# One hybrid layer on one core: the feed-forward variances on GpSimd, the channel mixes and three feed-forwards summed by VectorE, and new orders

## The reference, cut to what matters

```python
x = hidden                                     # (8, 512, 128): 8 batches, 512 tokens, 128 channels
n = layernorm(x);  q = n @ W_q.T               # attention without softmax
x = x + (q @ n.T) @ n
x = x + ffn(layernorm(x))
x = x + rwkv_block(layernorm(x))               # token mix (a scan over tokens), then channel mix
x = x + ffn(layernorm(x))                      # the same weights as the first feed-forward
def ffn(y):                                    # only expert 0 has weight
    z = y + relu(y @ w1 + b1) @ w2 + b2
    return (z - mean(z)) * rsqrt(var(z) + 1e-5) * gamma + beta
def channel_mix(x, xc):                        # second half of the rwkv block
    k = square(relu(mix(xc) @ Wk.T))
    return x + sigmoid(mix(xc) @ Wr.T) * (k @ Wv.T)
```

## Time and profile before

| what | value |
|---|---|
| median of 3 runs | 259.32 us |
| the profiled execution's own time | 259.21 us |
| its span | 257.4 us |
| TensorE busy | 249.5 us, 97% |
| VectorE busy | 231.2 us, 90% |
| ScalarE busy | 231.9 us, 90% |
| GpSimd busy | 133.2 us, 52% |
| granted TensorE clock | 0.997 of full |

### The profile page before, as it was taken

The page is one execution under the profiler, slowest core; times in us unless marked ns, Lnnn a source line. Parts: engine busy times, 40 slices in busy tenths (PEclk is TensorE's granted clock), DMA queues, the critical chain, the costliest instruction groups (busy, mean ns, idle before and its releaser), DMA issues.

```text
span 257.4 us, 5284 instructions
## 1 busy us (share of the span) xinstructions
PE 249.5 (97%) x1504; PEld 187.8 (73%) x1504; DVE 231.2 (90%) x757; ACT 231.9 (90%) x477; POOL 133.2 (52%) x258
## 2 busy tenths in 40 slices
PE   7899999999999999999999999999999999999991
PEld 7687778768767777668759767757848849778771
DVE  5897999999999999999999999999999995955454
ACT  3789789999999999999999999999999999895741
POOL 1656585944961974044596646636604525340640
PEclk9999999999999999999999999999999999999998
DMA  7932224013022240020763422205204424374297
GB/s 196 308 99 45 42 42 84 0 28 56 3 40 43 41 84 1 0 45 0 134 105 52 74 48 45 42 0 98 67 0 85 81 56 70 55 144 87 45 187 179
DMA packets 17772, 18.10 MB, mean 70 GB/s; under 512 B 1488, under 2 KB 11600, under 8 KB 17744
## 3 DMA queue, kind: packets, MB, share of 16 engines
q0 software_dynamic: 6480, 11.80, 27.0%
q1 hardware_dynamic: 10848, 5.84, 8.1%
q10 hardware_dynamic: 416, 0.14, 0.2%
HBM read 3.87 MB, written 2.10 MB: 23 GB/s over the span
## 4 chain that ended last, share of the span: by engine, by line
PE 94%; DVE 2%; DMA 1%; ACT 1%; POOL 1%; issue 0%; DVEq 0%; POOLq 0%; ACTq 0%
PE bank L1155 21%; PE bank L1164 21%; PE bank L1232 11%; PE bank L1226 11%; PE bank L1114 7%; PE bank L1213 3%; PE bank L1243 3%; PE bank L1197 3%; PE bank L1207 3%; PE bank L1202 3%; PE bank L1142 3%; PE bank L1127 2%; PE bank L1275 1%; DMA R<-in_hidden 1%; PE bank L1175 1%; PE bank L1135 1%
## 5 line engine op out<-in xcount | busy, mean ns | idle before, releaser
L1164 PEld LDWEIGHTS bank<-W,f_h 128*128 128x128 f32 x480 | 58.2, 192 | 8.7 <-issue 8.6
L1155 PE MATMUL bank<-f_yT,W 128*128 128x512 f32 x128 | 61.2, 593 | 0.0
L1164 PE MATMUL bank<-W,f_h 128*128 128x128 f32 x480 | 60.2, 275 | 0.0
L1155 PEld LDWEIGHTS bank<-f_yT,W 128*128 128x128 f32 x128 | 21.9, 190 | 16.3 <-issue 11.3
L1232 PEld LDWEIGHTS bank<-FWv,KK 128*128 128x128 f32 x256 | 30.6, 192 | 3.4 <-issue 2.3
L1226 PE MATMUL bank<-XK,FWk 128*128 128x512 f32 x64 | 32.0, 597 | 0.0
L1232 PE MATMUL bank<-FWv,KK 128*128 128x128 f32 x256 | 31.8, 275 | 0.0
L828 ACT ACTIVATE f_y<-R,f_yn_nb,f_yn_rs 128x128 f32<-128x128 f32 x64 | 26.3, 490 | 0.9 <-POOL f_yn_nb L350 0.9
L895 ACT ACTIVATE f_h<-bank,B 128x512 f32<-128x512 f32 x32 | 21.2, 681 | 5.5 <-PE bank L1155 4.2
L390 POOL DMA_DIRECT2D R<-G x7 | 6.3, 897 | 36.4 <-DVE G L686 36.4
L895 ACT ACTIVATE f_h<-bank,B1C 128x512 f32<-128x512 f32 x32 | 21.4, 682 | 0.1
(11 more groups left out here) (159 smaller groups left out, 620.3 us busy)
## 6 DMA issues: line engine op xcount, KB each, us to landing
R<-BETA POOLq DMA_DIRECT2D x16, 256.0 KB, 3.6
R<-f_zg POOLq DMA_DIRECT2D x14, 256.0 KB, 4.0
R<-N POOLq DMA_DIRECT2D x8, 256.0 KB, 3.4
R<-in_hidden SPq DMA_DIRECT2D x7, 256.0 KB, 5.0
R<-G POOLq DMA_DIRECT2D x7, 256.0 KB, 3.4
out_x<-R SPq DMA_DIRECT2D x7, 256.0 KB, 2.3
W<-in_w SPq DMA_DIRECT2D x2, 256.0 KB, 4.5
BETA<-in_beta SPq DMA_DIRECT2D x1, 256.0 KB, 4.6
```

Source lines behind the costliest of these rows:

```text
L1155: t_.matmul(banks[bank][:], W1[:, n * P:(n + 1) * P], at(f.yT, b)[:], start=True, stop=True).then_inc(f.h_psum[n], 1)
L1164: last = t_.matmul(banks[bank][:, j * C:(j + 1) * C], at(f.h, b)[:, n, j * P:(j + 1) * P], W2[:, n, :], start=False, stop=(n == H - 1), sk ...
```

## The change

It does four things.

1. `mean_var` of the 15 unsplit z goes from VectorE. In its place GpSimd runs `z_spread`: four small instructions that join the two halves of `bn_stats` to C times the variance. The logarithm reads that with `scale=1/C`. The wait of `z_stats` for its buffer is now on that step.
2. The seven accumulating DMAs of the channel mix and three of the feed-forwards (batch 4 of f1, batches 5 and 6 of f2) go from GpSimd's queue. VectorE adds instead: `cmix_out` for all batches, and a new `ffn_add`.
3. All four lists (GpSimd, VectorE, ScalarE, TensorE) have a new order and new banks. No matmul is added or removed.
4. One constant tile more is set at the start, so that the count waited for goes from 8 to 9.

```diff
-ADDED = {"f1": (0,), "f2": (7,), "x3": (7,)}
+ADDED = {"f1": (0, 4), "f2": (5, 6, 7), "x3": tuple(range(BATCHES))}
...
+            def z_spread(b, n):
+
+                pool.wait_ge(n.stats_done, b + 1)
+                if b >= 2:
+                    pool.wait_ge(*n.scale.done(b - 2, "ve"))
+                st = n.stats[b % 2]
+                pool.tensor_tensor(n.pair[b % 2][:], st[:, :, 1], st[:, :, 4], ALU.mult).then_inc(n.scale.sem(b), 1)
+                pool.tensor_tensor(n.sum[b % 2][:], st[:, :, 2], st[:, :, 5], ALU.add)
+                pool.wait_ge(*n.scale.done(b, "pair"))
+                pool.tensor_tensor(n.pair[b % 2][:], n.pair[b % 2][:], K_C[:], ALU.mult).then_inc(n.scale.sem(b), 1)
+                pool.wait_ge(*n.scale.done(b, "scaled"))
+                pool.tensor_tensor(n.spread[b % 2][:], n.sum[b % 2][:], n.pair[b % 2][:], ALU.subtract).then_inc(n.scale.sem(b), 1)
...
-            def cmix_sum(b):
-
-                pool.wait_ge(*cgate.done(b, "kvs"))
-                pool.wait_ge(*x2u.ready(b))
-                for earlier in x3.before(b):
-                    pool.wait_ge(*earlier)
-                pool.dma_start(R[b][:], at(G2, b)[:].rearrange("p (j c) -> p j c", j=J), accum_op=ALU.add).then_inc(*x3.step(b))
...
+            def ffn_add(b, f, tile):
+
+                dve.wait_ge(f.zg_ready, b + 1)
+                dve.wait_ge(*f.xb.ready(b))
+                v.tensor_tensor(R[b][:], at(tile, b)[:], R[b][:], ALU.add).then_inc(*f.out.step(b))
...
-                act.wait_ge(n.mv_ready, b + 1)
+                act.wait_ge(*n.scale.done(b, "spread"))
...
-                a.activation(n.ve[b % 2][:], n.mv[b % 2][:, :, 1], ACT.Ln, bias=K_EPS[:, 0:1]).then_inc(n.scale.sem(b), 1)
+                a.activation(n.ve[b % 2][:], n.spread[b % 2][:], ACT.Ln, bias=K_EPS[:, 0:1], scale=1.0 / C).then_inc(n.scale.sem(b), 1)
```

The beginning and the end of TensorE's list, the beginning of GpSimd's and the end of ScalarE's and VectorE's, which the prediction follows:

```diff
-            attn_transpose(0, 0); attn_gram(0, 1); attn_proj(0, 1); attn_apply(0, 1); attn_transpose(1, 0)
-            attn_gram(1, 2); attn_transpose(2, 1, x1.ready(0)); attn_proj(1, 2); attn_gram(2, 3); bias_rows()
-            attn_apply(1, 2); attn_transpose(3, 1); attn_proj(2, 3); attn_gram(3, 4)
-            ffn_transpose(0, f1, 2, x1.ready(1)); attn_apply(2, 3); hidden_up(0, f1, 0, 2)
+            attn_gram(0, 0); attn_transpose(0, 1); attn_proj(0, 0); attn_apply(0, 0); attn_transpose(1, 1)
+            attn_gram(1, 2); attn_transpose(2, 0, x1.ready(0)); attn_proj(1, 2); attn_gram(2, 3); attn_apply(1, 2)
+            attn_proj(2, 3); bias_rows(); ffn_transpose(0, f1, 0); attn_apply(2, 3); hidden_up(0, f1, 1, 0)
...
-            power(3, na); shift(0, f1.norm); bias(3, na); power(0, f1.norm); bias(0, f1.norm); shift(1, f1.norm)
+            power(3, na); shift(0, f1.norm); power(0, f1.norm); bias(0, f1.norm); shift(1, f1.norm); power(1, f1.norm)
...
-            proj_evacuate(0, 1); attn_normed(1); attn_normed(2); gram_evacuate(1, 2); attn_evacuate(1, 0)
-            attn_evacuate(2, 1); proj_evacuate(1, 2); attn_normed(3); gram_evacuate(2, 3); ffn_normed(0, f1)
+            proj_evacuate(0, 0); attn_normed(1); attn_normed(2); gram_evacuate(1, 2); attn_evacuate(1, 1)
+            attn_evacuate(2, 0); proj_evacuate(1, 2); gram_evacuate(2, 3); ffn_normed(0, f1); proj_evacuate(2, 3)
...
-            ffn_evacuate(7, f2, 5); z_root(5, f2.znorm); relu(7, f2, 0, 5); z_log(6, f2); z_root(6, f2.znorm)
-            relu(7, f2, 2, 0); relu(7, f2, 1, 4); relu(7, f2, 3, 5); last_log(0); last_root(0); last_log(1)
+            z_log(5, f2); ffn_evacuate(7, f2, 7); z_root(5, f2.znorm); z_log(6, f2); z_root(6, f2.znorm)
+            relu(7, f2, 0, 1); relu(7, f2, 1, 2); relu(7, f2, 3, 7); relu(7, f2, 2, 5); last_log(0); last_root(0)
...
-            last_start(0, 6); ffn_scaled(5, f2, 0); z_stats(6, f2, 3); last_start(1, 1); mean_var(6, f2.znorm)
-            ffn_scaled(6, f2, 3); last_stats(0, 6); last_scaled(0, 6); last_mean_var(0); last_stats(1, 1)
+            last_start(0, 3, (f2.h_ready[3], 7)); z_stats(6, f2, 4); ffn_scaled(5, f2, 5); ffn_add(5, f2, f2.zg)
+            last_start(1, 6); ffn_scaled(6, f2, 4); ffn_add(6, f2, f2.zg); last_stats(0, 3); last_scaled(0, 3)
```

More of the change, by code:

```diff
@@ L139, in __init__ @@
                 self.rs = copies(n + "_rs", [P, J], 2)
+                if "spread" in steps:
+                    self.pair, self.sum, self.spread = (copies(n + "_" + m, [P, J], 2) for m in ("pair", "sum", "spread"))
                 self.stats_done = sem(n + "_stats_done")
@@ L404, in _ @@
[L404 to L408, removed]
@@ L437, in row_stats @@
                 if b >= 2:
-                    dve.wait_ge(n.mv_ready, b - 1)
+                    if n in (f1.znorm, f2.znorm):
+                        dve.wait_ge(*n.scale.done(b - 2, "spread"))
+                    else:
+                        dve.wait_ge(n.mv_ready, b - 1)
                 for j in range(J):
@@ L469, in last_stats @@
                 dve.wait_ge(*last[part].done(0, "z"))
-                dve.wait_ge(f2.znorm.mv_ready, B - 2)
+                dve.wait_ge(*f2.znorm.scale.done(B - 3, "spread"))
                 stats_rows(f2.znorm, B - 1, bank_rows(bank), LAST[part], last[part].sem(0))
@@ new lines, in _ @@
+            differences(2, 0); mix_r(2); cmix_k(0); tmix_out(1, 7); z_stats(4, f1, 4); tmix_stats(3); cmix_stats(1)
+            cmix_r(0); mean_var(3, nt); denominator_sum(2); attn_out(7, 7); mean_var(1, ncm); new_values(2, 0)
+            ffn_scaled(4, f1, 4); numerator_sum(2); ffn_stats(7, f1); first_values(2, 0); weighted(2)
+            ffn_add(4, f1, f1.zg); with_current(2); mean_var(7, f1.norm); gate_sum(2); tmix_stats(4); tmix_change(3)
+            mean_var(4, nt); mix_k(3); gate_log(2, 2); cgate_log(0, 6); cmix_change(1); gated(2); cmix_k(1)
@@ new lines, in _ @@
+            ffn_transpose(1, f1, 0, (f1.h_ready[3], 1)); ffn_down(0, f1, 2, 1); ffn_down(0, f1, 3, 1); attn_gram(3, 4)
+            attn_transpose(3, 0, (f1.yT_ready, 2)); hidden_up(1, f1, 2, 7); hidden_up(1, f1, 0, 1, (f1.zg_ready, 1))
+            hidden_up(1, f1, 3, 4, (gram_ready, 4)); attn_proj(3, 5); ffn_transpose(2, f1, 2); attn_transpose(4, 6)
+            hidden_up(1, f1, 1, 5, (proj_ready, 4)); attn_apply(3, 0); ffn_down(1, f1, 0, 3); ffn_down(1, f1, 1, 3)
+            tmix_transpose(0, 0, x1.ready(3)); ffn_down(1, f1, 2, 3); ffn_down(1, f1, 3, 3)
@@ new lines, in _ @@
+            attn_transpose(5, 1); hidden_up(3, f1, 1, 3, (m2_ready, 1)); hidden_up(3, f1, 2, 7, (xa_ready, 2))
+            attn_gram(6, 2, (proj_ready, 6)); bias_part(0, (f1.h_ready[0], 4)); ffn_down(3, f1, 0, 6)
+            product_k(1, 1, (xnT_ready, 6)); hidden_up(3, f1, 3, 3); ffn_down(3, f1, 1, 6)
+            product_v(1, 2, (gram_ready, 7)); ffn_transpose(4, f1, 4, gate.done(0, "rl")); ffn_down(3, f1, 2, 6)
+            attn_apply(5, 0, (b1_ready, 1)); attn_proj(6, 3, (f1.h_ready[3], 4))
```

484 lines of the change are left out of this document (242 added, 242 removed).

## The result

The changed kernel takes 262.96 us (median of 4 runs, 262.49 to 264.0), the kernel before 259.31 us beside it. The ratio is 1.0138, 95% interval 1.0119 to 1.0157. The prediction was 259.1 us, with a range to 260.8 us. It was wrong, on the slower side. The profiled execution took 262.49 us with a span of 260.7 us, 3.3 us over the span before. Of all executions reported here, one, of the run with eight extra additions from SBUF, took 922.36 us for a reason that its record doesn't show, and its ratio leaves that one out.

The account below looks back on a forecast made before the run. TensorE was taken as the bound, busy for 97% of the span, with about 1.7 us of waits to win. 259.21 + 0.45 (start) - 0.3 (earlier f2 work) - 0.25 (end) = 259.1 us, range 257.9 to 260.8 us.

Parts of the forecast that it names:

- VectorE's load in sum: Whole kernel: 5.5 us of `bn_aggr` leave VectorE, ten additions bring 6.9 us, so 1.4 us more.
- The first Gram matrix: Start of TensorE's work: it comes ahead of the first transposes, near 6.3 us, not 6.70, after 0.4 us idle.
- The walk of the end: Last batches and stores: last issue 0.3 us earlier, less DMA sharing 0.1, later ReLUs and `last_start(1)` cost 0.15; -0.25 us.
- the start: To 34 us: waits before the first f1 transpose and from moved norms and copies, +0.45 us, ends 0 and +1.0.
- The middle: The new order between start and end, not walked: 0 us beside the earlier f2 work, ends -1.4 and +1.5 us.
- earlier f2 work: Channel-mix sums by VectorE instead of DMA give TensorE f2 work some 3.6 us earlier, worth 0.3 us.
- The late variance: Rival: late `z_spread` on in-order GpSimd holds `z_log`, ScalarE and a PSUM bank of TensorE; 260.5 us, chance 0.14.
- VectorE is the bound: Rival: before 200 us VectorE is nearly full, its 1.4 us more moves token mixes, TensorE waits; 260.2 us, chance 0.09.
- the port rule: VectorE with two SBUF inputs and GpSimd reading SBUF lock each other; `z_spread` beside an addition up to 0.7 us longer.
- the sign that I had named: Feed-forward outputs: `z_log` would come less than 1.2 us behind `z_stats` in the median.
- The other sign: TensorE: the prediction is wrong if its waits after 12 us are far from 2 us.
- The clock: Rival: 0.4 us idle before the first Gram matrix could delay TensorE's clock rise; +1.4 us, 260.5 us, chance 0.05.

## Why the prediction was wrong, point by point

**What held.** VectorE's load in sum (+1.5 us against +1.4). The first Gram matrix, at 5.99 us (6.3 foreseen, the load came earlier). The walk of the end: `z_log(6)` ahead of batch 7's ReLUs, `last_start(1)` behind `ffn_add(5)`, and the last stores right behind `last_out`:

```profile
251.10 0.30 ACT L1036 ACTIVATE f_zn_ve<-f_zn_spread,K_EPS 128x4 f32<-128x4 f32 x1 [2.94 <-POOL f_zn_spread L358]
251.22 0.69 DVE L587 TENSOR_TENSOR R<-f_zg,R 128x512 f32<-128x512 f32 x1
...
252.26 2.15 SPq L243 DMA_DIRECT2D out_x<-R  x3
...
257.36 1.13 DVE L506 SCALAR_TENSOR_TENSOR R<-f_zg,f_zn_rs,R 128x128 f32<-128x128 f32 x4
...
257.99 0.90 SPq L270 DMA_DIRECT2D out_x<-R  x2
```

Its size was too small: -0.25 us taken, -0.8 us in the trace, and -0.9 to -1.05 us with one addition alone.

**Right by luck.** I took +0.45 us for the start, and the gaps to 40 us are 0.9 us longer, inside 0 to +1.0. But the waits that I had walked aren't there: up to 20 us nothing is lost, and of the 0.4 us ahead of the first f1 transposes (15.14 us) 0.12 us are found. The 0.96 us from 20 to 40 us come from the late variance of batch 1 (the rows at 38 us) and are 0.00 us in both runs of the new lists without `z_spread`. They belong to a rival's price.

**The step that failed** is "The middle. [...] I take 0", with "-0.3 (earlier f2 work)" beside it. TensorE's gaps from 40 to 200 us grew by 3.3 us, over twice the upper end of +1.5. I had put the new order at nothing because the distances in the lists "look alike", and the additions at nothing because I had netted them. The late variance, with a step of 1.0 us worked out for it, has no term in the sum at all. Three things are in the loss.

1. The lists. With both parts out they cost 0.8 us net. The old lists without the `bn_aggr` take 258.7 us, and the end wins 0.9 to 1.05 us, so 257.7 us is my estimate for old lists with both parts out (that run wasn't made). Against it the new lists cost about 2.5 us, probably the largest of the three. In the trace the gaps lie at 48.7, 64.6 and 141.3 us, the last behind the GpSimd order shown above. The new order pays for itself only by what it saves of `z_spread`'s lateness.

2. The additions, 1.6 us in the new lists, 4.4 us in the old. I counted them only as a net load of 1.4 us, against the `bn_aggr` taken away, and then left even that out of the sum. Before, VectorE was busy for all of the middle:

```profile
40.00:200.00 160.00, 160.00 (x953) 117.76 (x952) 159.49 (x458) 158.32 (x310) 89.18 (x156) 1.00 0.27 47
```

An addition there costs 0.5 us (runs with eight extra ones, with two late ones). The relief was mis-sized too: the 60 `bn_aggr` are 5.5 us as a group, but leaving them out lowers VectorE's busy time by 3.7 us (231.2 to 227.5), and wins 0.7 us alone. Beside the additions it is worth 2.5 us, since they have made gaps that it can fill. "VectorE is the bound" was the rival that came true in part, priced from the wrong number; its 260.2 us also takes off the 0.3 us of earlier f2 work, which is in the 259.1 already.

3. The late variance, the other rival, came true with them: 1.1 to 1.3 us in the new lists, 3.0 us in the old. I had taken 1.0 us for the step "since the median sits at the low end". From the start of its first instruction to the end of its fourth `z_spread` took 0.78 to 5.65 us, 1.29 in the median and 1.57 in the mean; its instructions are 198 to 205 ns in the median but 401 in the mean, with 16 of 60 over 260 ns. The trace of before could have told: its 149 small instructions of this size have a mean of 348 ns. I had applied the port rule to the ten new additions alone, while VectorE's scans and elementwise work from SBUF were there all along. By the trace the logarithm starts 1.0 and 2.0 us behind `z_stats` for batches 0 and 1, against 0.5 before. In the median over all 15 it is 4.3 against 4.6 us, since most logarithms have other work ahead of them: the sign that I had named, less than 1.2 us in the median, was a poor one. The other sign told: TensorE's waits after 12 us, 2.4 us before, are 6.6 us.

The earlier f2 work didn't show anywhere: the eight extra additions, with all DMAs kept, cost 3.8 us, and the real sums, with the DMAs gone and the gain of the end in them, 4.4 us.

**The clock** played no part. The profile gives a granted clock of 1.00 in every stretch from 0 to 250 us before, the warm-up too, so the change of level that I named isn't in that column; it is in the pace. Before, matmuls start every 0.213 us up to 6.52 us and every 0.112 us from 6.70 us on. After, they start every 0.213 us up to 5.67 us and every 0.112 us from 6.18 us on, behind an idle of 0.2 us: the faster pace came 0.5 us earlier, not later, and the rival's 1.4 us aren't there (4.92 against 5.00 us of gaps to 20 us).

**Open.** Why a gap at 77 us is 0.36 us in the changed kernel's profile and 1.0 to 1.2 us in three others with the same or nearly the same lists to there. It may be why that kernel's runs lie 1.5 us apart and those of before 0.6 us; that is argued, not shown. What the 1.5 us are that the eight real additions cost over the eight extra ones. And which moves in the new lists make their 2.5 us; the one move taken back won 1.0.

## What to carry to other kernels

When two engines are both full, price first what an edit adds: an instruction more costs most of its length. Then give the relief at most the gaps that it can fill, 0.7 us here alone and 2.5 us beside the additions. Don't put a new order at nothing because it can't be walked; here it was probably the largest term, and a run of the new lists with the parts cut out shows it. Price small instructions that wait for another engine by their mean, not their median. Read an engine's room at the place where the instruction will stand, not from the busy share of 20 us around it. The cheap part of a large edit may be the good one: one addition at the end, where VectorE stood waiting, won 0.4%, and the whole change lost 1.4%.

## What the runs showed of the hardware

GpSimd's small instructions are held by VectorE, depending on where its inputs are. Of the kernel before I took the 149 instructions of 128 by 4 numbers but for the powers, by what VectorE was doing when they started (statistics that read PSUM count under PSUM):

| VectorE then | count | median ns | over 260 ns |
|---|---|---|---|
| elementwise or scan, all inputs in SBUF | 33 | 702 | 30 |
| an input in PSUM | 58 | 198 | 8 |
| `bn_stats`, `bn_aggr` | 45 | 198 | 2 |
| nothing, or other | 13 | 199 | 1 |

Twelve of the 149 started while GpSimd's own DMA issue was under way, and all twelve took 474 ns or more: six of the first row, five of the second, one of the last. Without them the rows have 24 of 27, 3 of 53, 2 of 45 and 0 of 12 over 260 ns, so what the first row shows doesn't rest on them.

The changed kernel gives 44, with a median of 644 ns and 40 over 260 ns, in the first row; its row of statistics has 17 of 67 over 260 ns, eight of them under an own DMA issue; some of the others end with an operation from SBUF that starts next. This agrees with the Trainium skill ("SBUF — State Buffer", the section on the two separate sides), which has VectorE with two SBUF inputs and a GpSimd instruction that reads SBUF lock one port pair against each other. A hold can be longer than one instruction: behind a DMA issue and two scans it was 2.3 us (2.5 us for 0.2, at 136.57 us). VectorE paid nothing that shows: before, its scans took 1.19 to 1.22 us, whether or not a GpSimd instruction was under way when they started.
